# Second attention: a batch's output product as three f16 products, with the split shared by ScalarE and GpSimd

## What is computed

```
q = l @ Wq                              # l: normalized x, 4 x 512 x 128
kv = concat([norm(ctx), l], 1) @ Wkv    # 154 + 512 rows, 2 x 1024 columns
w = softmax(q k^T / 8)                  # 16 heads of 64
out = (w @ v) reshaped to 512 x 1024
x = layernorm(x + out @ Wo)             # Wo: 1024 x 128
```

## Time and profile before

| | us |
|---|---|
| runs shown: median, lowest, highest | 1605.43, 1594.52, 1605.57 |
| profiled execution, its own time | 1597.89 |
| its span, from the first to the last instruction | 1596.1 |
| PE busy in it | 1451.0 |
| DVE, ACT, POOL busy | 1125.7, 925.6, 694.8 |

### The profile page before, as it was taken

One profiled execution on the slowest core, in us unless ns is written; L12 is line 12 of the kernel. 1 busy time (PEld: TensorE's weight loads), 2 busy tenths in 40 slices (PEclk: granted clock), 3 DMA queues, 4 the chain that ended last, 5 costly groups with the idle time before them and its releaser, 6 DMA issues.

```text
span 1596.1 us, 44182 instructions
## 1 busy us (share of the span) xinstructions
PE 1451.0 (91%) x19224; PEld 800.5 (50%) x19224; DVE 1125.7 (71%) x2297; ACT 925.6 (58%) x1301; POOL 694.8 (44%) x741
## 2 busy tenths in 40 slices
PE   8888888899999999999988988999999989999996
PEld 4222222343434334333434544787877778775453
DVE  6778877888877885867727668576777765574654
ACT  2788775787867876887672443555455544342220
POOL 2111131566655665676580108457776567010000
PEclk9999999999999999999999999999999999989898
DMA  4000003333322341332302000000000002000000
GB/s 166 1 1 1 1 1 108 106 95 91 95 77 77 91 109 52 104 91 78 94 6 79 1 1 14 16 17 17 4 17 17 17 3 67 28 2 1 8 7 14
DMA packets 32417, 70.80 MB, mean 44 GB/s; under 512 B 5328, under 2 KB 7056, under 8 KB 31968
## 3 DMA queue, kind: packets, MB, share of 16 engines
q1 hardware_dynamic: 32224, 67.98, 14.5%
HBM read 47.45 MB, written 20.51 MB: 43 GB/s over the span
## 4 chain that ended last, share of the span: by engine, by line
PE 62%; ACT 14%; DVE 14%; issue 7%; POOL 2%; DMA 0%; ACTq 0%; DVEq 0%; SPq 0%; POOLq 0%
PE ps L160 60%; ACT b_X L961 3%; ACT a_E L470 3%; DVE b_mx L899 2%; ACT b_EH L169 2%; POOL b_EL L979 1%; DVE a_MX L433 1%; PE ps L242 1%; ACT b_Hk L169 1%; PE ps L1598 1%; DVE b_Lk L840 1%; ACT b_OT L169 1%; DVE X L234 1%; DVE st L172 1%; DVE b_rd L1072 1%
## 5 line engine op out<-in xcount | busy, mean ns | idle before, releaser
L979 POOL TENSOR_TENSOR b_EL<-b_X,b_EH 128x1024 f16<-128x1024 f32 x160 | 341.1, 2132 | 193.5 <-ACT b_EH L169 193.3
L961 ACT ACTIVATE b_X<-ps 128x1024 f32<-128x1024 f32 x160 | 163.7, 1023 | 88.6 <-PE ps L160 86.8
L1784 POOL TENSOR_TENSOR d_tmp<-d_G,d_XI 128x31 f32<-128x31 f32 (+15 forms) x248 | 126.5, 510 | 162.6 <-DVE d_G L1713 143.7
L433 DVE TENSOR_REDUCE a_MX<-ps 128x2 f16<-128x1024 f32 x128 | 155.3, 1227 | 45.7 <-PE ps L160 45.3
L169 ACT ACTIVATE b_EH<-b_X 128x1024 f16<-128x1024 f32 x160 | 169.1, 1057 | 26.0 <-PE ps L160 14.8
L899 DVE TENSOR_REDUCE b_mx<-ps 128x2 f32<-128x1024 f32 x128 | 155.9, 1218 | 37.0 <-PE ps L160 35.1
L160 PE MATMUL ps<-b_M,b_S 128*64 128x512 f16 (+1 forms) x1408 | 175.6, 381 | 3.4 <-ACT b_X L961 3.3
L470 ACT ACTIVATE a_E<-ps 128x1024 f32<-128x1024 f32 x128 | 131.1, 1024 | 49.2 <-PE ps L160 49.0
L1787 POOL TENSOR_TENSOR d_XI<-d_XI,d_tmp 128x31 f32<-128x31 f32 (+15 forms) x248 | 139.6, 563 | 19.4
L160 PEld LDWEIGHTS ps<-b_M,b_S 128*64 128x64 f16 (+1 forms) x1408 | 70.9, 108 | 80.3 <-ACT b_X L961 14.1
L452 POOL TENSOR_TENSOR a_QS<-a_QS,a_MR 128x512 f16<-128x512 f16 x16 | 18.5, 1156 | 201.0 <-ACT a_MR L169 197.1
(11 more groups left out here) (323 smaller groups left out, 3322.3 us busy)
## 6 DMA issues: line engine op xcount, KB each, us to landing
b_S<-s_xk SPq DMA_DIRECT2D x48, 336.0 KB, 6.3
b_M<-s_xq SPq DMA_DIRECT2D x48, 256.0 KB, 5.0
s_xk<-b_Hk SPq DMA_DIRECT2D x16, 336.0 KB, 2.2
s_xk<-b_Lk SPq DMA_DIRECT2D x16, 336.0 KB, 2.5
s_xq<-b_Hq SPq DMA_DIRECT2D x16, 256.0 KB, 2.0
s_xq<-b_Lq SPq DMA_DIRECT2D x16, 256.0 KB, 2.0
d_XI<-eye SPq DMA_DIRECT2D x8, 512.0 KB, 3.8
f_w<-f_w SPq DMA_DIRECT2D x1, 2048.0 KB, 8.7
```

Source lines behind the costliest of these rows:

```text
L433: v.e.tensor_reduce(out, PS[:, bk:bk + 2, :], AX, ALU.max).then_inc(sem("a_mx"), 1)
L961: a.e.activation(b_X[k % 2], PS[:, bk:bk + 2, :], ACT.Exp, scale=0.125).then_inc(sem("b_ex"), 1)
L979: last = p.e.tensor_tensor(b_EL[k % 6], b_X[k % 2], b_EH[k % 6], ALU.subtract)
L1784: e.tensor_tensor(tm, a, x, ALU.mult).then_inc(*p.step())
```

## The change

The output product is made from f16 parts. `Wo`, scaled by 16, is split once into a high and a low part by POOL, in the first stage (`b_split_out_gpsimd`, three operations of 128x1024). The 8 tiles of a batch are split too: ACT copies tile k to f16 (`b_high_scalar`), POOL subtracts (`b_rest_gpsimd`). PE then makes three f16 products (high x high, high x low, low x high) where it made one f32 product: 96 matmuls of 128 columns per batch for 32. DVE's add divides by 16. The parts of tile k are laid over tile k-1 (those of tile 0 over a new buffer `b_OS`), so copy k waits until tile k-1 has been subtracted (semaphore `b_ol`). Copies stand in eight consecutive slots behind `b_EH` (x.10 of the unit before, then 0 to 6), the subtractions behind the `b_EL` of slots 0 to 7, and the product moves from slot 7 to slot 9.

```diff
+        b_wo = r0.take("b_wo", 1024, F16).rearrange("p (k a n) -> p k a n", k=2, a=8)
+        b_fo = Room(nc, 44064).take("b_fo", 1024).rearrange("p (a n) -> p a n", a=8)
...
+        b_OS = rB.take("b_OS", 512)
...
+        def b_split_out_gpsimd(p):
+            e = p.e
+            p.wait_ge("ld_w1", 96)
+            e.tensor_scalar(b_fo, b_fo, B_OUT_UP, None, ALU.mult).then_inc(*p.step())
+            p.wait_own()
+            e.tensor_copy(b_wo[:, 0], b_fo).then_inc(*p.step())
+            p.wait_own()
+            e.tensor_tensor(b_wo[:, 1], b_fo, b_wo[:, 0], ALU.subtract).then_inc(sem("b_wos"), 1)
...
+        def b_parts(b, a):
+            x = b_OT[b % 2][:, a - 1, :] if a else b_OS
+            return x.bitcast(F16).rearrange("p (k n) -> p k n", k=2)
+
+        def b_high_scalar(a, b, k):
+            a.wait_ge("b_sel", 8 * b + k + 1)
+            a.wait_ge("b_ol", 8 * b + k)
+            a.wait_ge("b_out", b)
+            copy(a.e, b_parts(b, k)[:, 0], b_OT[b % 2][:, k, :]).then_inc(sem("b_oh"), 1)
+
+        def b_rest_gpsimd(p, b, k):
+            P = b_parts(b, k)
+            p.wait_ge("b_oh", 8 * b + k + 1)
+            p.e.tensor_tensor(P[:, 1], b_OT[b % 2][:, k, :], P[:, 0], ALU.subtract).then_inc(sem("b_ol"), 1)
...
-            yield
+            for _ in range(3):
+                yield
             bo = banks.take(t, ("bo", b), 1, "b_add", b + 1)
-            t.wait_ge("b_sel", 8 * b + 8)
+            t.wait_ge("b_wos", 1)
+            t.wait_ge("b_ol", 8 * b + 8)
             for j in range(4):
                 for a in range(8):
-                    last = mm(e, PS[:, bo, 128 * j:128 * j + 128], O[:, a, 128 * j:128 * j + 128], b_wo[:, a, :],
-                              start=(a == 0), stop=(a == 7))
+                    P = b_parts(b, a)
+                    for op, wp in ((0, 0), (0, 1), (1, 0)):
+                        last = mm(e, PS[:, bo, 128 * j:128 * j + 128], P[:, op, 128 * j:128 * j + 128], b_wo[:, wp, a, :],
+                                  start=(a == 0 and op + wp == 0), stop=(a == 7 and op == 1))
...
-            add_vector(v, b, bank["bo", b], "b_add")
+            stt(e, xb(b), PS[:, bank["bo", b], :].rearrange("p (a b) -> p a b", a=4), 1.0 / B_OUT_UP, xb(b),
+                ALU.mult, ALU.add).then_inc(sem("b_add"), 1)
...
-        B_OUT = 25
+        B_OUT = 27
...
         def b_out_scalar(a, b):
-            yield from later(B_OUT, ())
+            for _ in range(4):
+                yield
+            for k in range(8):
+                b_high_scalar(a, b, k)
+                yield
+            yield from later(B_OUT - 12, ())
...
                     b_low_gpsimd(p, u, s)
+                    b, k = divmod(11 * (u + 2) + s - 77, 44)
+                    if b >= 0 and k < 8:
+                        b_rest_gpsimd(p, b, k)
+            for k in range(8):
+                b_rest_gpsimd(p, NB - 1, k)
...
-            weave((tail, 35), (both(experts(lane, 0, begun), part(second, 4)), 13))
+            weave((tail, 37), (both(experts(lane, 0, begun), part(second, 4)), 13))
...
         def d_clear_gpsimd(p):
 
+            p.wait_ge("b_out", 4)
```

More of the change, by code:

```diff
@@ L30 @@
     "f_bm": ("a_oc", 16), "f_xm": ("a_pv", 64),
-    "d_inv": ("a_ws", 4), "d_x1": ("b_kv", 6), "d_btm": ("b_kt", 6), "xr_E": ("xr_A", 4), "xr_F": ("xr_B", 4), "f_wh": ("d_wh", 3), "f_xb": ("a_xb", 4),
+    "d_inv": ("a_ws", 4), "d_x1": ("b_kv", 6), "d_btm": ("b_kt", 6), "xr_E": ("xr_A", 4), "xr_F": ("xr_B", 4), "f_wh": ("d_wh", 3), "b_oh": ("ld_cst", 16), "b_ol": ("ld_wm", 32), "b_wos": ("ld_xt0", 16), "f_xb": ("a_xb", 4),
 }
@@ L642, in a_gpsimd @@
                     a_bias_gpsimd(p, G // 4)
+                if G == 8:
+                    b_split_out_gpsimd(p)
                 if G == 12:
@@ L657, in build @@
         b_wq, b_wk, b_wv = (r0.take(n, 1024) for n in ("b_wq", "b_wk", "b_wv"))
-        b_wo = r0.take("b_wo", 1024).rearrange("p (a n) -> p a n", a=8)
+        B_OUT_UP = 16.0
+        b_wo = r0.take("b_wo", 1024, F16).rearrange("p (k a n) -> p k a n", k=2, a=8)
+        b_fo = Room(nc, 44064).take("b_fo", 1024).rearrange("p (a n) -> p a n", a=8)
         b_ln = r0.take("b_ln", 5)
@@ L700, in b_load_sync @@
         def b_load_sync(s):
-            for o, i in ((b_wq, "x_wq"), (b_wk, "x_wk"), (b_wv, "x_wv"), (b_wo, "x_wo"), (b_sel, "b_sel"), (c_sel[0:48], "c_sel")):
+            for o, i in ((b_wq, "x_wq"), (b_wk, "x_wk"), (b_wv, "x_wv"), (b_fo, "x_wo"), (b_sel, "b_sel"), (c_sel[0:48], "c_sel")):
                 dma(s.e, "ld_w1", o, io[i])
+        def b_split_out_gpsimd(p):
[6 more added lines that the diff above has]
+            e.tensor_tensor(b_wo[:, 1], b_fo, b_wo[:, 0], ALU.subtract).then_inc(sem("b_wos"), 1)
         B_KEYS = (("c", 0), ("l", 0), ("l", 1), ("c", 1), ("l", 2), ("l", 3))
@@ L1041, in b_den_vector @@
             last.then_inc(sem("b_dn"), 1)
+        def b_parts(b, a):
[10 more added lines that the diff above has]
+            p.e.tensor_tensor(P[:, 1], b_OT[b % 2][:, k, :], P[:, 0], ALU.subtract).then_inc(sem("b_ol"), 1)
         def b_out_tensor(t, b, banks=ringP):
-            e, O = t.e, b_OT[b % 2]
+            e = t.e
             for _ in range(4):
@@ L1229, in b_tail_scalar @@
         def b_tail_scalar(a):
-            yield from later(1 + B_OUT + 6, ())
+            yield from later(2, b_out_scalar(a, NB - 1))
+            for _ in range(5):
+                yield
             turn_scalar(a, "B", NB - 1)
```

## The result

The changed kernel takes 1687.45 us (median of 5 runs, 1681.39 to 1693.55), the kernel before 1605.43 (median of 5, 1594.52 to 1608.83). The ratio is 1.0516, interval 1.0479 to 1.0553: slower, 7.4 us above the predicted 1680.1 and within its range.

What follows compares the result with a forecast made beforehand. PE was taken as the bound (1451.0 of 1596.1 us busy). Base 1597.9 + 77.1 (three middle batches, each +25.6 - 1.9 + 2) + 5.1 (tail) = 1680.1 us, range 1655 to 1705 us.

Steps and rivals of the forecast that it cites:

- The loop: Middle batches: ACT's copies 1 to 7 each wait for POOL's b_EL and subtraction, seven turns; chain 25.6 us longer per batch.
- the rival of 1658 us: Middle batches: the loop is there, but two of seven turns are hidden, 18.4 us per batch; chance 0.12.
- the sum: The adding up for middle batches: 4.06 us per copy, 28.4 for seven, less 2.8 of ACT's waits for PE.
- The clock: Middle batches: PE falls to 1.2 GHz after idling, slowing pieces that stay in the chain; 2 us per batch taken.
- the bounds: Limits set on the middle batches' cost; PE's lower clock could add up to 7 us per batch.
- the three places that the sum named: Where half clock matters: projection to b_EH at 608.05, scores before 611.35, the product's start; 2 us per batch taken.
- The product: A middle batch's output product on PE: 96 f16 pairs at 0.06 us, 5.8 us for 7.70, saving 1.9.
- The sum of the middle: Batches 0 to 2: +25.7 us each from loop, product and clock, +77.1 us for three.
- the base: The profiled execution of the kernel before, 1597.89 us, to which the terms were added; the median is 1605.43.
- The tail: Batch 3, among the next stage's experts: product starts 6.5 us later and is 1.4 us shorter, +5.1 us.
- What costs nothing: The split of Wo (under 6.4 us, in POOL's 10.39 us idle), DVE's add and the product's move by two slots: free.
- The rival "only themselves": Middle batches and tail: copies cost only their own work, -1.0 us per batch, tail -1.4, 1593 us; chance 0.06.

Runs made afterwards that it cites:

- e4: The changed kernel with 16 more zero-weight matmuls of 512 columns in PE's idle in slots 1, 3, 4 and 7 of units 5, 9 and 13; 1684.23 us.
- e1: The changed kernel with POOL's order turned round: each subtraction ahead of the b_EL of its slot instead of behind it; 1608.64 us, ratio 1.0025.
- e2: The changed kernel with the parts of tile k over tile k-2, so copy k waits for subtraction k-2; 1608.06 us, ratio 1.0007.
- e3: The changed kernel with every subtraction done twice on POOL; 1712.89 us, ratio 1.0675.
- e12: e11 for batches 0 to 2, with batch 3's tail exactly as in the changed kernel (f16 product, copies among the experts); 1599.14 us, ratio 0.9959.
- e11: e10 with copies behind the projection's copy, ahead of exponentials that wait for PE, and subtractions ahead of b_EL; 1599.34 us, ratio 0.9965.
- e8: e2 with middle copies and subtractions in idle places, parts three tiles apart, tail's copies, product and add two steps later, old weaving; ratio 1.0049.
- e10: e2 with middle copies and subtractions in idle places, parts three tiles apart, batch 3 unsplit (f32 product, old tail order); 1605.69 us, ratio 1.0018.

## Why the prediction was right

- **The loop** is the mechanism as forecast, and all seven turns wait; none is hidden (the rival of 1658 us). The wait is 3.40 us for 3.43 in the sum; ACT's next operation starts 3.94 us after `b_EH`'s end (628.55 against 624.61), forecast 3.96. Measured for the whole: stretch 59.7 - 30.2 = 29.5 us per batch, less 3.7 for the clock by e4 = 25.8, forecast 25.6. e1 and e2 show that the wait makes it, with the lower clock that comes with PE's idle: without the wait 2.8 us of the 29.5 are left (e2, 33.0 for 30.2). e3 shows that the wait's length counts one for one. One reading in the sum was off: the wait of 1.06 us before the `b_EH` of slot 9.4 was taken as staying and is 2.02 (652.36), and 2.02 in e4 too, because PE's projection there waits for DVE's `b_Lq` and so for the `b_Hq` behind copy 4:

```profile
650.20 0.78 PE L160 MATMUL ps<-b_KV,b_wk 128*64 128x333 f32 x4 [1.22 <-DVE b_Lq L852]
```

- **The clock** is the term that was mis-sized: 3.7 us for the 2 taken. The serial pieces at 1.2 GHz were in the bounds (up to 7), and the value lay nearer their middle than I took. It also lay elsewhere. Of the three places that the sum named, only the scores of slot 9.5 paid (1 us, by e4); the `b_EH` of slot 9.4 waits as long in e4, and the product took 57 ns a pair, at a granted clock of 1.00. The rest, 2.7 us, lies behind copy 7, in slots 9.8 and 9.9 (scores of 1.92 us for 1.03, 677.01 against 670.86), which the sum did not name.
- **The product** saves 7.70 - 5.46 = 2.24 us for the 1.9 taken; a pair costs 57 ns for 60. The Trainium skill's 81 ns ("TensorE: Matmul & The Clock Gate", "Back-to-back issue gap") give an estimate of 7.8 us; the measurement decides, and it follows the transposes of the earlier trace rows.
- **The sum of the middle**: 627.1 - 546.5 = 80.6 us, forecast 77.1. The whole rise was forecast as 82.2 us and is 82.0 in medians. That it fits to 0.2 us is luck: the middle alone is 3.5 us above its forecast, the tail's price can't be told in medians, and runs of one kernel spread over 12 to 14 us. The 7.4 us by which the time itself is off is the base, a profiled execution 7.5 us below its median.
- **The tail**: in the profile +6.7 us (43.5 for 36.8), forecast 5.1, the product 8.6 us later and 1.9 shorter (forecast 6.5 and 1.4). In medians the split tail cannot be told from none (e12). Whether the 5.1 us are real stays open; it is 6% of the loss.
- **What costs nothing**: up to the first scores the changed kernel's profile is 1.9 us behind; e2, e1 and e11, with the same split of `Wo`, stand at -2.3, 0.0 and 2.0 there, so it is the spread between executions and not the split.
- **The rival "only themselves"** (1593 us) is what the split comes to in an order in which nobody waits: it put the kernel 5 us under the one before, and e11 and e12 are 0.35% and 0.41% (6 us) under it.
- PE's share in the stretch was forecast near half and is 0.64 (38.18 of 59.73); exponentials were forecast 6 to 7 us apart and are 6.1 to 6.9, except one of 11.5 us, where ACT waits twice for PE (652.36 and 660.77).

## What to carry to other kernels

Work that "fits" by busy shares fits only if no one waits for it: walk the queues of the two engines and ask whether a copy waits for something that is queued behind work started by the instruction just ahead of it. Parts laid in place over the neighbour made such a circle here; a place one tile further off, or the other order on one engine, cut it and gave back 79 us. Put added work behind what others want and ahead of an instruction that waits anyway: only in that order (e11, e12) did the shorter product show in the time.

## What was not expected of the hardware

Some of DVE's operations within SBUF stand still while POOL subtracts. In e8 POOL made three subtractions from 859.78 (its row: sum of three), and DVE's small operations meanwhile:

```profile
859.78 3.44 POOL L1074 TENSOR_TENSOR b_OT<-b_OT 128x512 f16<-128x512 f32 x3 [0.71 <-ACT b_OT L169]
```

```profile
859.01 0.16 DVE L1380 TENSOR_SCALAR c_wt<-c_wt 128x4 f32<-128x4 f32 x1
...
859.62 0.23 DVE L1386 TENSOR_TENSOR c_oh<-iota,c_ixf 128x64 f32<-128x64 f32 x1
...
859.90 1.12 DVE L1388 TENSOR_SCALAR c_wt<-c_wt 128x8 f32<-128x8 f32 x1
861.06 1.13 DVE L1390 TENSOR_TENSOR c_oh<-c_oh,c_wt 128x64 f32<-128x64 f32 x1
862.11 1.19 DVE L1391 TENSOR_TENSOR c_oh<-c_oh,c_wt 128x64 f32<-128x64 f32 x1
```

The operation at 859.90 takes 1.12 us, the two behind it 1.13 and 1.19; their kind took 0.16 and 0.23 us just ahead, at 859.01 and 859.62. DVE's products that read PSUM kept their 0.68 us: ten of e8's `b_OT<-b_OT,ps` stood beside a subtraction and took 0.68 to 0.69 us. Nor does every operation within SBUF wait: in the changed kernel a search (`FIND_INDEX8`, 938.34) took its 0.17 us beside the subtraction of 938.20. The Trainium skill bears on this ("SBUF — State Buffer", "SBUF: two separate sides"): GpSimd shares a port pair with those DVE operations that have two SBUF inputs or run in a two-port mode; whichever starts first holds it for its whole instruction, and the other "fully blocks". The trace agrees as to the blocking, 1.12 us being about one subtraction's 1.15.

And the same tail in the same order took 47.5 or 52.5 us to its tenth `c_SG`, by the moment at which PE's clock fell (e10 and e11 above).
